# The last group of a residual pass: half-group moments and powers, centring ahead of the power, scale and residual in one operation

## What is computed

```python
    x = x + _layernorm(_L0_attn_ref(_layernorm(x, axis=-1), ...), axis=-1)
    x = x + _layernorm(_L0_ffn_ref(_layernorm(x, axis=-1), ...), axis=-1)

def _layernorm(x, axis=-1, eps=1e-05):
    m = jnp.mean(x, axis=axis, keepdims=True)
    v = jnp.var(x, axis=axis, keepdims=True)
    return (x - m) / jnp.sqrt(v + eps)
```

## Time and profile before

| | us |
|---|---|
| median of 3 runs | 1089.59 |
| lowest and highest of them | 1089.08 and 1089.89 |
| the profiled execution, its own time | 1089.17 |
| span of its instructions, first to last | 1087.4 |

### The profile page before, as it was taken

The page is one execution under the profiler, slowest core; times in us unless marked ns, Lnnn a source line. Parts: engine busy times, 40 slices in busy tenths (PEclk is TensorE's granted clock), DMA queues, the critical chain, the costliest instruction groups (busy, mean ns, idle before and its releaser), DMA issues.

```text
span 1087.4 us, 19513 instructions
## 1 busy us (share of the span) xinstructions
PE 1047.9 (96%) x6863; PEld 958.0 (88%) x6863; DVE 656.2 (60%) x1714; ACT 503.7 (46%) x895; POOL 385.4 (35%) x347
## 2 busy tenths in 40 slices
PE   7998999999999999999999999999999999999985
PEld 6886888888888888889887899999999999999875
DVE  7768864677753678754786334545545463635686
ACT  4343444443434444353463334554546363545475
POOL 3112561114640104640117631434433343211385
PEclk9999999999999999999999999999999999999988
DMA  8222460242540234461134214434334242333799
GB/s 289 104 98 78 132 219 17 82 155 95 167 148 20 79 125 138 150 210 39 59 136 161 103 33 157 133 67 112 88 90 109 65 124 56 77 89 94 262 220 171
DMA packets 47229, 129.15 MB, mean 119 GB/s; under 512 B 10276, under 2 KB 17576, under 8 KB 47152
## 3 DMA queue, kind: packets, MB, share of 16 engines
q1 hardware_dynamic: 28656, 92.83, 25.5%
q0 software_dynamic: 18496, 35.35, 14.3%
HBM read 73.72 MB, written 54.40 MB: 118 GB/s over the span
## 4 chain that ended last, share of the span: by engine, by line
PE 82%; DVE 8%; POOL 4%; issue 3%; ACT 1%; DMA 1%; DVEq 0%; POOLq 0%; SPq 0%; ACTq 0%
PE bank L1136 25%; PE bank L1138 25%; PE bank L1137 25%; PE bank L1155 2%; POOL out_dram L906 2%; POOL sb_place_of L911 1%; DVE sb_stX L1427 1%; PE bank L1262 1%; PE bank L1315 1%; DVE sb_act L1734 1%; PE bank L1215 1%; PE bank L1274 1%; ACT sb_ln_o L965 1%; DMA sb_ysb<-in_L_ffn_W2s_dram 1%; PE bank L1185 1%
## 5 line engine op out<-in xcount | busy, mean ns | idle before, releaser
L1734 DVE TENSOR_TENSOR sb_act<-bank,sb_act 128x512 f32<-128x512 f32 (+2 forms) x240 | 148.6, 619 | 347.8 <-PE bank L1138 330.5
L1136 PE MATMUL bank<-sb_h_hi,sb_wup_lo 128*128 128x512 f32 (+2 forms) x960 | 354.7, 369 | 3.3 <-ACT sb_act L1061 2.1
L1138 PE MATMUL bank<-sb_h_hi,sb_wup_hi 128*128 128x512 f32 (+2 forms) x960 | 350.0, 365 | 0.0
L1137 PE MATMUL bank<-sb_h_lo,sb_wup_hi 128*128 128x512 f32 (+2 forms) x960 | 349.7, 364 | 0.0
L1061 ACT ACTIVATE sb_act<-bank 128x512 f32<-128x512 f32 (+2 forms) x240 | 129.8, 541 | 378.1 <-PE bank L1138 358.4
L1136 PE MATMUL bank<-sb_wdn_hi,sb_act_lo 128*128 128x256 f32 (+1 forms) x848 | 245.5, 290 | 5.1 <-ACT sb_ysb L1043 4.4
L1138 PE MATMUL bank<-sb_wdn_hi,sb_act_hi 128*128 128x256 f32 (+1 forms) x848 | 239.2, 282 | 0.0
L1137 PE MATMUL bank<-sb_wdn_lo,sb_act_hi 128*128 128x256 f32 (+1 forms) x848 | 239.0, 282 | 0.0
L1136 PEld LDWEIGHTS bank<-sb_h_hi,sb_wup_lo 128*128 128x128 f32 x960 | 181.0, 189 | 24.4 <-DVE sb_act L1734 2.5
L1138 PEld LDWEIGHTS bank<-sb_h_hi,sb_wup_hi 128*128 128x128 f32 x960 | 180.6, 188 | 22.6
L1137 PEld LDWEIGHTS bank<-sb_h_lo,sb_wup_hi 128*128 128x128 f32 x960 | 181.2, 189 | 17.1
(11 more groups left out here) (265 smaller groups left out, 1238.5 us busy)
## 6 DMA issues: line engine op xcount, KB each, us to landing
sb_xin<-in_L_ffn_W_dram SPq DMA_DIRECT2D x28, 512.0 KB, 3.6
sb_x<-in_L_attn_x_dram SPq DMA_DIRECT2D x16, 512.0 KB, 3.7
out_dram<-sb_x SPq DMA_DIRECT2D x16, 512.0 KB, 3.4
sb_xin<-in_L_attn_x_dram SPq DMA_DIRECT2D x14, 512.0 KB, 4.6
sb_xin<-in_x_turned_dram SPq DMA_DIRECT2D x14, 512.0 KB, 4.3
y_scratch<-sb_ysb SPq DMA_DIRECT2D x14, 512.0 KB, 4.2
sb_xn<-in_L_ffn_W_dram SPq DMA_DIRECT2D x14, 512.0 KB, 4.4
hT_scratch<-sb_hr SPq DMA_DIRECT2D x12, 512.0 KB, 2.7
```

The costliest lines, as they stand in the source:

```text
L1136: t_.matmul(o, a_lo, b_hi, start=start, stop=False, skip_group_check=True)
L1137: t_.matmul(o, a_hi, b_lo, start=False, stop=False, skip_group_check=True)
L1138: return t_.matmul(o, a_hi, b_hi, start=False, stop=stop, skip_group_check=True)
L1734: v.tensor_tensor(act[:, m % 3, 0:c.w], bank[(4 if c.wide and m % 2 else 0) + 1][:, 0:c.w], act[:, m % 3, 0:c.w], ALU.mult).then_inc(act_o ...
```

## The change

VectorE handles group 15 in two halves, each with its own moments and its own eps addition, so `t_var` is raised twice and GpSimd makes two powers of two rows each (`last_rstd(CLOSE, ...)`, 128x2 in place of 128x4). Half 0 goes on as before: bias on VectorE, normalised by ScalarE, added to `close_x` by VectorE. Half 1 has no bias: VectorE subtracts the mean while the power is awaited, and then one `scalar_tensor_tensor` for each row multiplies by the scale and adds the row of `close_x`. Half 0 is stored first. GpSimd makes both powers before it issues the accumulate of group 14; those of 12 and 13 still go first.

```diff
-            for h in (1, 0):
-                sp.wait_ge(t_half, 2 - h)
+            for h in range(2):
+                sp.wait_ge(t_half, h + 1)
                 sp.sem_inc(sp_go, 1)
                 sp.dma_start(out_t[CLOSE][:, 2 * h:2 * h + 2, :], close_x[:, 2 * h:2 * h + 2, :]).then_inc(t_end, 16)
...
-            for g in range(NG):
-                pool.wait_ge(t_var, g + 1)
-                v.tensor_tensor(t_scale[g % SLOTS], t_ve[g % SLOTS], mhalf[:, :], ALU.pow).then_inc(t_rstd, 1)
+            def last_rstd(g, cut, count):
+                pool.wait_ge(t_var, count)
+                v.tensor_tensor(t_scale[g % SLOTS][:, cut], t_ve[g % SLOTS][:, cut], mhalf[:, cut], ALU.pow).then_inc(t_rstd, 1)
+
+            for g in range(CLOSE):
+                last_rstd(g, slice(0, GT), g + 1)
...
-                if 3 <= g < CLOSE:
+                if g >= 3:
                     last_sum(g - 3)
-                if g == CLOSE - 1:
-                    for late in range(CLOSE - 3, CLOSE):
-                        last_sum(late)
+            for late in (CLOSE - 3, CLOSE - 2):
+                last_sum(late)
+            for h in range(2):
+                last_rstd(CLOSE, slice(2 * h, 2 * h + 2), NG + h)
+            last_sum(CLOSE - 1)
...
+            def close_sum(h):
+                dve.wait_ge((dn_half, dn_done)[h], (1, OPEN + NCH * FM)[h])
+                half = flat4(y[:, 2 * h:2 * h + 2, :])
+                v.tensor_tensor(half, half, bank[2 + h][:, :], ALU.add).then_inc(t_sum, 1)
+                dve.wait_ge(t_sum, HELD + h)
+                for t in (2 * h, 2 * h + 1):
+                    ins = v.bn_stats(st[:, t, :], y[:, t, :])
+                ch.link(ins)
+
+            def close_moments(h):
+                for t in (2 * h, 2 * h + 1):
+                    ins = v.bn_aggr(t_mv[slot_of][:, t, :], st[:, t, :])
+                ch.link(ins)
+                cut = slice(2 * h, 2 * h + 2)
+                v.tensor_scalar(t_ve[slot_of][:, cut], t_mv[slot_of][:, cut, 1], EPS, None, ALU.add).then_inc(t_var, 1)
+
+            dve.wait_ge(t_y[CLOSE % TY], 16 * (CLOSE // TY + 1))
+            close_sum(0)
+            close_moments(0)
+            close_sum(1)
+            dve.wait_ge(t_rstd, NG)
+            v.scalar_tensor_tensor(out=t_bias[slot_of][:, 0:2], in0=t_mv[slot_of][:, 0:2, 0], scalar=-1.0,
+                                   in1=t_scale[slot_of][:, 0:2], op0=ALU.mult, op1=ALU.mult).then_inc(t_nb, 1)
+            close_moments(1)
+            for t in (2, 3):
+                ins = v.tensor_scalar(y[:, t, :], y[:, t, :], t_mv[slot_of][:, t, 0:1], None, ALU.subtract)
+            ch.step(ins)
             dve.wait_ge(t_x, 16)
-            for h in (1, 0):
-                dve.wait_ge((t_act, t_sum)[h], (NG, HELD + 2)[h])
-                half = slice(2 * h, 2 * h + 2)
-                v.tensor_tensor(flat4(close_x[:, half, :]), flat4(close_x[:, half, :]), flat4(y[:, half, :]),
-                                ALU.add).then_inc(t_half, 1)
+            dve.wait_ge(t_act, NG)
+            v.tensor_tensor(flat4(close_x[:, 0:2, :]), flat4(close_x[:, 0:2, :]), flat4(y[:, 0:2, :]),
+                            ALU.add).then_inc(t_half, 1)
+            dve.wait_ge(t_rstd, NG + 1)
+            ch.settle()
+            for t in (2, 3):
+                ins = v.scalar_tensor_tensor(out=close_x[:, t, :], in0=y[:, t, :], scalar=t_scale[slot_of][:, t:t + 1],
+                                             in1=close_x[:, t, :], op0=ALU.mult, op1=ALU.add)
+            ins.then_inc(t_half, 1)
```

More of the change, by code:

```diff
@@ L1804, in _ @@
                             ALU.mult).then_inc(t_idx, 1)
[L1806 to L1810, removed]
             def last_stats(g):
@@ L1814, in last_stats @@
                 dve.wait_ge(t_y[g % TY], 16 * (g // TY + 1))
-                if g == CLOSE:
-                    last_half(g, 0)
-                elif GROUP[g] == FIRST:
+                if GROUP[g] == FIRST:
                     dve.wait_ge(y_sb, OPEN + NCH - HELD + 1)
@@ L1827, in last_moments @@
                 ch = Chain(dve, t_chain, 2 * g)
-                if g == CLOSE:
-                    last_half(g, 1)
                 for t in range(GT // 2, GT):
@@ L1855, in _ @@
             last_pass(HELD_PLACES)
[L1856 to L1864, removed]
-            dve.wait_ge(t_x, 16)
@@ L1866, in _ @@
-            for h in (1, 0):
-                dve.wait_ge((t_act, t_sum)[h], (NG, HELD + 2)[h])
-                half = slice(2 * h, 2 * h + 2)
-                v.tensor_tensor(flat4(close_x[:, half, :]), flat4(close_x[:, half, :]), flat4(y[:, half, :]),
-                                ALU.add).then_inc(t_half, 1)
+            y, slot_of = last_y[CLOSE % TY], CLOSE % SLOTS
+            ch = Chain(dve, t_chain, 2 * CLOSE)
+            def close_sum(h):
[6 more added lines that the diff above has]
+                ch.link(ins)
```

## The result

The changed kernel takes 1091.33 us (median of 9 runs, 1090.28 to 1092.73) against 1089.40 of the kernel before on the same chip (9 runs): a ratio of 1.0019, 95% interval 1.0010 to 1.0027. It is slower by some 2 us, and outside the predicted range.

A forecast was written before the change was run, and what follows sets the result against it. The prediction took the DMA engines' work to bound the last 12 us. With 2.7 + 1.34 = 4.05 us of work left from 1082.1 in both kernels, the sum was 0.0 and the forecast 1089.6 us, range 1088.7 to 1090.8.

The forecast's parts named there:

- The place: Last 12 us of the kernel: bound by the DMA engines' work, not by the chain of engines the change shortens.
- land at 1087.0, as before. The sum is 0.0: End of the kernel: last data end at 1086.15 and land at 1087.0 as before, a change of 0.0 us.
- So the engines do not run idle: DMA engines from 1082.1: stores fill the time until the last accumulate's data flow, 4.05 us of work in both kernels.
- Rival two: Last accumulate, behind half 1's power on GpSimd, becomes the last to land: 1.4 us slower, 1091.0; chance 0.20.
- Rival one: Stores overtake the accumulates on the DMA queues: 0.9 us faster, 1088.7; chance 0.17 together with another rival.
- the centring: VectorE subtracting half 1's mean: 0.73 us beside half 1's power, ending at 1079.5.
- Half 1's power: GpSimd's second power, of two columns: 1.15 us, from 1078.84 to 1080.0, with the last accumulate issued at 1080.2.
- the two fused operations: VectorE's scaling and addition for half 1's rows: 0.75 us, high bound 0.9, ending at 1081.05.
- The rules: Ports shared by VectorE and GpSimd: no loss taken for the centring; if it held them, half 1's power 0.73 us later.

The follow-up runs named there:

- E4: The changed kernel with both stores of group 15 held back until group 13's accumulate has landed; 1089.28 us, ratio 1.0003 to the kernel before.
- E6: The changed kernel with groups 13 and 14 stored plainly after VectorE adds their residual, instead of accumulated; 1087.33 us, ratio 0.9981 to the kernel before.
- E7: The kernel before, without halves, with groups 13 and 14 stored plainly instead of accumulated; 1087.73 us, ratio 0.9984.
- E3: The kernel before with its single power of group 15 ahead of the accumulate of group 14; 1090.16 us, ratio 1.0009.
- E2: The changed kernel with the accumulate of group 14 issued between the two powers; 1090.55 us, ratio 1.0003 to the kernel before.

## Why the prediction was wrong

**What held.** The place: the last 12 us are bound by the transfers, and the shorter chain of engines is worth nothing there. Powers, centring, additions and stores ran in the order given, and the stores left 1.6 and 1.4 us sooner from F (predicted 1.44 and 1.25).

**The steps that failed** are the two that close its section on the DMA engines.

*"land at 1087.0, as before. The sum is 0.0".* This took the last landing for the end, with the same rest behind it whoever lands last: 0.9 us for the accumulate and 0.8 for the stores, both read from data to landing. (By the ends of the packets it is 0.3 for both, and the data end 0.5 us later than the prediction has it; the two errors cancel.) What follows the landing was left out, and it is not the same: 1.63 us behind an accumulate, 0.47 behind a store. The accumulate was allowed to land 1.3 us later for nothing; it had 0.1. The difference of the two rests, 1.16 us, would have made the sum +1.2 with all else as predicted. The table of waits could have warned only by what it lacks: the accumulate landed at 1085.7, and nothing in the earlier trace rows says what GpSimd does from there to the end.

*"So the engines do not run idle".* The stores would fill the time until the accumulate's data flow, so the last data would end as before. By their packets the stores did take the 1.34 us counted (shares of 55.2, 73.8 and 8.7% of the three microseconds from 1081 on, so 1.38). But they cost the accumulate 2.05 us (E4 against after). Part of the other 0.67 is the hole from 1083 to 1084 us; the rest I have not placed. Nor was there a gap to fill: by the packets the accumulate's data follow group 13's at F+7.93 in E4, while in the changed kernel they start at F+9.01 and need 4.3 us instead of 3.3. In the frame of F the last landing was due at 12.57 and came at 13.69: 1.1 us. With the 1.16 us of the rest this is the whole 2.3.

**Rival two** had the right mechanism and sign: the last accumulate last to land, with the stores ahead of its data. Its conditions were wrong. It was to need slow powers and an issue from 1080.6 on (F+6.2); it came with an issue at F+5.08, sooner than forecast. Nor does its price follow from the prediction's own terms: by them the stores are through at 1083.4 (1082.1 + 1.34), so the end moves only from an issue at 1081.1 on (2.3 us ahead of that), and one at 1081.2 lands at 1087.1, not 1088.4. That it named a loss of about the right order is in part luck. The range built on its 1.4 us was too small for the same reason as the sum, the missing exit. **Rival one** was right that the stores would overtake, which landed them at F+10.47 (it said by 1085, F+10.57), but not on what follows.

**Sizes.** Half 1's power took 0.73 us, not 1.15, and began 0.24 us sooner from F, so the accumulate was issued 2.2 us later from F, not 2.9; the two fused operations took 0.88 (0.75, bound 0.9); the centring 0.61 (0.73). Against the gain on GpSimd, the issue of the accumulate took 2.04 us instead of 1.54.

**The rules.** The centring did not hold the power up, since 0.73 us is within 0.01 of the shortest seen; nor did the addition of a PSUM bank (E6's first power, 0.72 us, lies beside one). An addition of two SBUF inputs that was already running did: the power ends 0.9 us behind the addition's end in the earlier trace rows (1059.75 to 1060.65) and in E7 (1079.43 to 1080.34). One that started during a power did not: E6's second power took 0.73 us, though the addition of group 14 began 0.35 us after it. This is as the Trainium skill has it, SBUF — State Buffer, section "Who interferes with whom", with `tensor_scalar` outside the two-port modes here.

The accumulate's issue goes the same way. Of the 130 issues of accumulates in the nine traces, all take 1.54 to 1.62 us but those that start while such an operation of VectorE has over 0.3 us left: 1.80 us with 0.33 us left (all nine traces have one), 2.04 with 0.57 (line 1883; after and E4), 2.21 with 0.79 (the 1024 columns of E6 and E7). E3's, with the additions starting 0.9 us after it, took 1.60. So 0.5 of the 2.04 us is the rest of half 0's addition. The same section of the Trainium skill remarks that `tensor_tensor` did not stall transfers in the probe that it reports; the issues here, which also read a tile of indices, were held up by one, as the rows above show.

## What to carry to other kernels

Ask of each engine what it still has to do behind its last landing: an accumulate issued by GpSimd late in a program is paid for until GpSimd's drain, here 1.63 us behind its landing against 0.47 for a plain store, and neither the chain nor the waits show that while another transfer lands last. Where an edit moves a transfer back in its queue so that a shorter one can start early, count which of the two the program can afford to have last. Here the bound by transfers was loosened by making them cheaper (plain stores in place of accumulates, 2 us) and not by feeding them earlier.

## What was unexpected of the hardware

- GpSimd's drain ends 1.404 us behind the last accumulate's landing with 15 accumulates in the program, 1.364 with 14 and 1.323 with 13: some 0.04 us for each, the same to 0.001 us in all kernels of one count.
- The power of two columns takes 0.72 to 0.73 us beside the centring or the addition of a PSUM bank; that of four takes 1.01 us at the least.
- Early stores are not kept waiting by the software queue always. Before, no packet of theirs ran until it was nearly dry (F+10.28); after, they ran from F+7.71 on, as group 13's packets ran out. This fits the prediction's condition that an accumulate's whole share on an engine is one piece, with the queues served by turns between pieces. E2 does not fit it: group 14 was queued by then, and both queues ran side by side. What decides this stays open.
